# Attention operands of 73 rows without fills, laid out by dimension, with the query loads regrouped

## The chip, the cores and the metric

The kernel runs on one core of a Trainium2 chip. The metric is the time of one execution on the device in microseconds (us). The kernel before takes 661.42 us, the median of 3 runs (659.46 to 661.67). A difference of about 0.3% (2 us) is what a measurement of this kernel can tell from no change.

## The reference

One transformer layer on x of 2048 tokens x 128 features, with 16 heads of 8 dimensions. `mod` has six rows of 128 numbers, computed from a conditioning vector.

```
h = layernorm(x) * (1 + ca) + sa
v = log_map(h)                                   # per token: sqrt, arccosh, a scale
q, k, vv = v @ Wq.T, v @ Wk.T, v @ Wv.T          # 16 heads of 8
g = eta + 0.1 * tanh(tanh((h - mu) @ W1.T + b1) @ W2.T + b2)      # abs, sign kept
at = softmax((q * g) @ k.T / sqrt(8))            # per head, 2048 x 2048
x = x + ga * project(project(mu) + 0.1 * (at @ vv) @ Wo.T)
h = layernorm(x) * (1 + cb) + sb
x = x + gb * ((silu(h @ wg.T) * (h @ wu.T)) @ wd.T)
```

## The kernel before

Preparation. DVE, ACT, GpSimd and PE compute h, the log map (DVE lines L910 to L964, on a [128, 16] array of one number per token and in between with ACT's roots and Ln), the metric g, and k, v and q, in four blocks of 512 tokens (BT). The head has only 8 dimensions and the scores need more accuracy than bf16, so k and q are each split into three bf16 parts (hi, mid, lo), and all nine products of parts are summed in one matmul: the contraction runs over 3 x 3 x 8 = 72 rows.

Operands. `K_op` [128, 16 heads, 2048] holds at row 24a + 8s + i, and `Q_op` [128, 2 slots x 16 heads x 512] at row 8 (3a + s) + i, what must be multiplied for the pair of parts (a, s) and the dimension i. One row more, SHIFT_ROW = 96, carries the softmax shift in Q_op against ones in K_op. Rows 72 to 95 of K_op are filled with zeros and 96 to 127 with ones by GpSimd (`fill_k`, L357 to L363, two memsets for each group of 4 heads), and rows 64 to 127 of both slots of Q_op with zeros (L373, L386). The memsets of groups 1 to 3 of K_op and of the first slot of Q_op lie beside DVE's log map.

The way of k and q. The parts have features on the rows, h * 8 + i. They go to memory: `store_k` (L241, one transfer of 128 rows for each block and part, on SP's queue), q of block 0 in one transfer on SP's queue (L277), q of blocks 1 to 3 on GpSimd's queue (L383). Back they come by SP's queue: `load_k(g)` loads a group of 4 heads in three transfers of 24 rows, since all three parts of k stand in every set of 24; `load_q` loads all 16 heads of one block in nine transfers of 8 rows, since each part of q stands three times; `load_shift` the shift row. SP's program is in order: stores of k, wait for them all, K of group 0, store of q, wait, queries of block 0, shift, K of groups 1 to 3, then queries of block 1, and then the gathers of results.

Attention. For each of 4 blocks of queries there are 64 steps, 16 for each group of 4 heads (GH). A step (`score`, L680) computes the scores of 128 keys against 512 queries for 4 heads with 16 matmuls at L700, each 32 keys wide and over 128 rows; ACT takes exp in two instructions of 128x1024 (L522); `product` (L708) multiplies the probabilities by the values in 4 matmuls (L716). In blocks 1 to 3 the output projection and the feed-forward part of the block before are spread over the steps (AT_WO to AT_DOWN). After block 3 the last tail runs by itself. PE begins block 0 when `Q_loaded` has all ten transfers of block 0 (L777), and each group of it when `K_loaded[g]` has its three (L685).

A second pass (p = 1) recomputes everything with exact shifts if a flag asks for it. With this data it isn't taken.

Of the kernel before, what the change touches and what calls it, by code (L numbers as in the profile page):

```python
# [29 lines left out]
DH = D // H  # L30
# [9 lines left out]
SHIFT_ROW = 96  # L40
# [18 lines left out]
ONE_PAIR = float(np.array([0x3F803F80], np.uint32).view(np.float32)[0])  # L59
# [16 lines left out]
def build(nc, x, columns, wmod, fixed, w1t, w2t, w_att, wgt, wut, wdt, out):  # L76
    with ExitStack() as ctx:
# [8 lines left out]
        k_scr = nc.dram_tensor("k_scr", (H, PARTS, DH, T), BF16, kind="Internal").ap()  # L86
# [118 lines left out]
        v_done kmax_ready bound shift_ready K_filled Q_filled Q_loaded ones_ready  # L205
        scores exped pv_done o_evac norm wo_ps h2_done h2T_ps h2T_done gate_ps up_ps gate_th
        gated glu_done down_ps y_ready y_stored tail epow_in epow_out flag_in flag_ps flag_ready placed exp_table warm num_in den_in
        max_loaded shift_saved max_zero max_scores max_taken max_T""".split()
# [6 lines left out]
        K_loaded = [sem(f"K_loaded{g}") for g in range(NG)]  # L215

        def q_slot(s):

            return lambda h: Q_op[:, bass.ds(s * (H * BT) + h * BT, BT)]
# [5 lines left out]
        QUERY_LOADS = PARTS * PARTS + 1  # L225
# [3 lines left out]
        def _(sp):  # L229
# [9 lines left out]


            def store_k(b):  # L241
                for n, part in enumerate(("k_hi", "k_mid", "k_lo")):
                    sp.wait_ge(S[part], b + 1)
                    sp.dma_start(k_scr[:, n, :, b * BT:(b + 1) * BT], k_parts[b % 3][:, n, :])\
# [26 lines left out]
            sp.wait_ge(S["K_filled"], 2)  # L271
# [32 lines left out]
            def blocks(p):  # L304
                for b in range(NB):
# [3 lines left out]
                    if b + 1 < NB:  # L309
                        if not p:  # L310
                            sp.wait_ge(q_st[b + 1], 16)
                            sp.wait_ge(S["shift_ready"], b + 2)
                            sp.wait_ge(S["Q_filled"], 2)
                        sp.wait_ge(S["Q_loaded"], 16 * QUERY_LOADS * (Bk + 1))
                        if Bk:
                            sp.wait_ge(S["scores"], 2 * STEPS * Bk)
                        load_q((b + 1) % 2, b + 1, S["Q_loaded"])
                        load_shift((b + 1) % 2, b + 1, S["Q_loaded"], p)
# [11 lines left out]
            with sp.If(sp.value_load(flag_i[0:1, 0:1], min_val=0, max_val=1)):  # L330
                sp.wait_ge(S["max_zero"], 1)
                for b in range(NB):
                    sp.wait_ge(S["max_taken"], NT * GH * b + 1)
                    load_q(0, b, S["max_loaded"])
                    sp.wait_ge(S["max_loaded"], 16 * PARTS * PARTS * (b + 1))
# [9 lines left out]
        def _(pool):  # L345
# [11 lines left out]
            def fill_k(g):  # L357

                hg = slice(GH * g, GH * (g + 1))
                pool.memset(K_op[64:96, hg, :].bitcast(F32), 0.0).then_inc(S["K_filled"], 1)  # L360
                pool.wait_ge(S["K_filled"], 2 * g + 1)
                pool.memset(K_op[96:128, hg, :].bitcast(F32), ONE_PAIR).then_inc(S["K_filled"], 1)  # L362
                pool.wait_ge(S["K_filled"], 2 * g + 2)  # L363

            pool.wait_ge(S["ones_ready"], 1)
            fill_k(0)

# [5 lines left out]
            pool.memset(Q_op[64:128, 0:H * BT].bitcast(F32), 0.0).then_inc(S["Q_filled"], 1)  # L373
            pool.wait_ge(S["Q_filled"], 1)
# [3 lines left out]
            for g in range(1, NG):  # L378
                fill_k(g)
# [5 lines left out]
            pool.wait_ge(S["m2_ps"], NB)  # L385
            pool.memset(Q_op[64:128, H * BT:2 * H * BT].bitcast(F32), 0.0).then_inc(S["Q_filled"], 1)  # L386
            pool.wait_ge(S["Q_filled"], 2)
# [9 lines left out]
            with pool.If(pool.value_load(flag_i[0:1, 0:1], min_val=0, max_val=1)):  # L397

                pool.memset(Q_op[96:128, 0:H * BT].bitcast(F32), 0.0).then_inc(S["max_zero"], 1)
                with pool.Fori(NB, 2 * NB) as b:  # L400
                    tail_roots(b)
# [3 lines left out]
        def _(act):  # L405
# [54 lines left out]
            def q_split1(b):  # L460
# [4 lines left out]
                if b == 3:  # L465
                    act.wait_ge(q_st[0], 16)
# [91 lines left out]
        def _(pe):  # L558
# [121 lines left out]
            def score(Bk, j):  # L680
# [3 lines left out]
                if kt == 0 and start:  # L684
                    pe.wait_ge(K_loaded[g], 16 * PARTS)  # L685
                queries = None if isinstance(Bk, int) else q_slot(Bk % 2)
                for half_ in range(2):
# [6 lines left out]
                    for i in range(2):  # L694
                        h = GH * g + 2 * half_ + i
                        if isinstance(Bk, int):
                            q_cols = Q_op[:, (Bk % 2) * H * BT + h * BT:(Bk % 2) * H * BT + (h + 1) * BT]
                            for c in range(COLS):
                                at_ = P * kt + CW * c
                                ins = pe.matmul(slot_bank(u % 3)[CW * c:CW * (c + 1), i, :],  # L700
                                                K_op[:, h, at_:at_ + CW], q_cols, start=True, stop=True,
                                                tile_position=(0, CW * c))
                        else:
                            ins = pe.matmul(slot_bank(u % 3)[:, i, :], K_op[:, h, P * kt:P * (kt + 1)], queries(h),
                                            start=True, stop=True)
# [50 lines left out]
            def block_steps(Bk, tails):  # L756
                for j in range(STEPS):
                    score(Bk, j)
# [16 lines left out]
            def blocks(p):  # L775
                first, last = NB * p, NB * (p + 1) - 1
                pe.wait_ge(S["Q_loaded"], 16 * QUERY_LOADS * (first + 1))  # L777
                block_steps(first, False)
                if p == 0:
                    pe.wait_ge(S["ffn_ready"], 3)  # L780
                if p == 0:
                    for Bk in range(first + 1, last + 1):
                        pe.wait_ge(S["Q_loaded"], 16 * QUERY_LOADS * (Bk + 1))
                        block_steps(Bk, True)
                else:
                    with pe.Fori(first + 1, last + 1) as Bk:
                        pe.wait_ge(S["Q_loaded"], 16 * QUERY_LOADS * (Bk + 1))
                        block_steps(Bk, True)
# [34 lines left out]
            with pe.If(pe.value_load(flag_i[0:1, 0:1], min_val=0, max_val=1)):  # L823

                q_all = q_slot(0)
                with pe.Fori(0, NB) as b:
                    pe.wait_ge(S["max_loaded"], 16 * PARTS * PARTS * (b + 1))
                    for h in range(H):
                        for t in range(TPB):
                            pe.wait_ge(S["max_taken"], b * (H * TPB) + h * TPB + t + 1)  # L830
                            for i in range(NB):
                                ins = pe.matmul(bank(i), q_all(h)[:, P * t:P * (t + 1)],
                                                K_op[:, h, BT * i:BT * (i + 1)], start=True, stop=True)
# [9 lines left out]
        def _(dve):  # L843
# [22 lines left out]
            vec.did(dve.memset(ones_bf[:, :], 1.0))  # L866
# [3 lines left out]
            for b in range(NB):  # L870
# [3 lines left out]
                if b == 1:  # L874
# [4 lines left out]
                    vec.after()  # L879
                    dve.tensor_scalar(silu_b[:, :], ones_bf[:, 0:P], silu_c[:, 0:1], c_c, ALU.mult, ALU.mult)\  # L880
# [388 lines left out]
```

## Time and profile before

| | us |
|---|---|
| median of 3 runs | 661.42 |
| runs | 659.46, 661.67, 661.42 |
| the profiled execution, its own time | 658.76 |
| its span, first to last instruction | 656.6 |
| PE busy | 569.7 (87%) |
| ACT busy | 527.0 (80%) |
| DVE busy | 163.4 (25%) |
| GpSimd (POOL) busy | 56.1 (9%) |
| mean granted clock of TensorE | 0.949 |

Busy times are sums over instructions in one profiled execution; a busy PE is not PE at its peak, since matmuls are pipelined. The granted clock is a share of full speed: 1.00 is 2.4 GHz and 0.50 is 1.2 GHz. The time outside the span is 2.2 us. PE is the tensor engine, PEld its weight loads, DVE the vector engine, ACT the scalar engine, SPq and POOLq the queues on which SP and GpSimd issue transfers.

### The profile page before, as it was taken

How to read it: one execution, taken by the hardware profiler on the slowest of the kernel's cores; microseconds unless marked ns; L12 is line 12 of the kernel's file. 1: busy time of each engine (PE TensorE's matmuls, PEld its weight loads, DVE VectorE, ACT ScalarE, POOL GpSimd, SP SyncE). 2: the span in 40 equal slices, each digit the busy share in tenths (PEclk: the TensorE clock that was granted, in tenths of full speed). 3: DMA queues.
4: the chain of work that ended last, by engine and by line, in shares of the span. 5: the costliest groups of instructions: out<-in, count | busy, mean ns of one | idle time of the engine just before them, and what ended most of it. 6: DMA issues, size and time to landing. Idle time of an engine off the chain costs nothing.

```text
span 656.6 us, 14893 instructions
## 1 busy us (share of the span) xinstructions
PE 569.7 (87%) x6482; PEld 210.6 (32%) x6482; DVE 163.4 (25%) x403; ACT 527.0 (80%) x607; POOL 56.1 (9%) x33
## 2 busy tenths in 40 slices
PE   1508832999999999999999999999999999999735
PEld 0305301333333333334333333333333333433213
DVE  7995650000000035110000451100005411010174
ACT  3325461999999999889999998899999988899601
POOL 6790040000000001000000000000000000000010
PEclk9967875999999999999999999999999999999959
DMA  5001577652000033000000330000000000000000
GB/s 162 0 0 36 126 126 135 108 77 31 10 2 9 2 44 40 10 1 10 17 10 1 51 35 8 2 9 18 9 3 9 5 6 1 10 18 9 1 0 20
DMA packets 16290, 19.30 MB, mean 29 GB/s; under 512 B 2112, under 2 KB 13568, under 8 KB 16224
## 3 DMA queue, kind: packets, MB, share of 16 engines
q1 hardware_dynamic: 15600, 16.76, 15.0%
q8 instruction: 52, 0.85, 0.5%
q0 software_dynamic: 336, 1.18, 0.5%
q10 hardware_dynamic: 288, 0.40, 0.2%
q14 instruction: 14, 0.11, 0.1%
HBM read 12.10 MB, written 4.19 MB: 25 GB/s over the span
## 4 chain that ended last, share of the span: by engine, by line
PE 49%; ACT 30%; DVE 8%; issue 7%; DMA 4%; POOL 0%; ACTq 0%; SPq 0%
ACT probs L522 28%; PE ps L716 19%; PE ps L700 18%; DMA Q_op<-wmod_sb 3%; PE ps L739 2%; PE ps L744 2%; PE ps L751 2%; PE ps L593 1%; DVE probs L924 1%; PE ps L725 1%; PE ps L587 1%; PE ps L613 1%; DMA x_tm<-x_dram 1%; DVE arena L921 1%; PE ps L676 1%
## 5 line engine op out<-in xcount | busy, mean ns | idle before, releaser
L522 ACT ACTIVATE probs<-ps 128x1024 f32<-128x1024 f32 x512 | 474.0, 1084 | 41.1 <-PE ps L700 41.0
L700 PE MATMUL ps<-Q_op,K_op 128*32 128x512 bf16 x4096 | 270.3, 381 | 19.5 <-DMA Q_op<-wmod_sb 18.9
L716 PE MATMUL ps<-probs,V_op 128*32 128x512 f32 x2048 | 272.2, 603 | 1.4 <-ACT probs L522 0.8
L700 PEld LDWEIGHTS ps<-Q_op,K_op 128*32 128x32 bf16 x4096 | 116.1, 97 | 222.8 <-issue 154.6
L1065 DVE COPY O_sb<-ps 128x512 f32<-128x512 f32 x16 | 11.1, 691 | 274.3 <-PE ps L716 274.3
L716 PEld LDWEIGHTS ps<-probs,V_op 128*32 128x32 f32 x2048 | 45.0, 108 | 94.1 <-ACT probs L522 85.4
L354 POOL TENSOR_TENSOR small<-small,half 128x4 f32<-128x4 f32 x4 | 4.1, 1014 | 519.3 <-DVE small L1118 519.3
L570 PE MATMUL ps<-fixed_sb,arena 128*128 128x128 f32 x32 | 7.4, 392 | 30.6 <-DVE arena L961 19.5
L428 ACT ACTIVATE small<-small 128x16 f32<-128x16 f32 x4 | 0.9, 216 | 23.2 <-DVE small L886 7.3
L1147 DVE SCALAR_TENSOR_TENSOR arena<-arena,ps 128x512 f32<-128x512 f32 x12 | 8.2, 687 | 43.5 <-ACT arena L537 43.5
L1153 DVE TENSOR_TENSOR arena<-ps,arena 128x512 f32<-128x512 f32 x12 | 8.3, 692 | 42.3 <-PE ps L744 42.2
L1165 DVE TENSOR_TENSOR arena<-ps,mod 128x512 f32<-128x512 f32 x3 | 2.1, 692 | 63.4 <-PE ps L751 63.4
L532 ACT ACTIVATE arena<-ps 128x512 f32<-128x512 f32 x4 | 2.4, 597 | 18.6 <-PE ps L732 18.6
L570 PEld LDWEIGHTS ps<-fixed_sb,arena 128*128 128x128 f32 x32 | 5.3, 198 | 34.3 <-DVE arena L961 20.4
L362 POOL MEMSET K_op<- 32x4096 f32 x4 | 14.0, 3506 | 0.2
L360 POOL MEMSET K_op<- 32x4096 f32 x4 | 14.0, 3504 | 0.3
L676 PE MATMUL ps<-ones_bf 128*128 128x512 bf16 x16 | 7.1, 613 | 7.8 <-POOL small L354 7.8
L1088 DVE RECIPROCAL arena<-arena 128x512 f32<-128x512 f32 x4 | 13.4, 3352 | 0.1
L739 PE MATMUL ps<-arena,wg_f 128*128 128x512 f32 x24 | 13.3, 636 | 0.0
L744 PE MATMUL ps<-arena,wu_f 128*128 128x512 f32 x24 | 13.2, 631 | 0.0
L537 ACT ACTIVATE arena<-ps 128x512 f32<-128x512 f32 x12 | 7.2, 597 | 6.9 <-PE ps L739 6.9
L751 PEld LDWEIGHTS ps<-wd_f,arena 128*128 128x128 f32 x72 | 8.9, 191 | 10.1 <-issue 10.1
(154 smaller groups left out, 299.9 us busy)
## 6 DMA issues: line engine op xcount, KB each, us to landing
K_op<-k_scr SPq DMA_DIRECT2D x12, 384.0 KB
Q_op<-q_scr SPq DMA_DIRECT2D x36, 128.0 KB
arena<-O_sb SPq DMA_DIRECT2D x120, 16.0 KB
k_scr<-probs SPq DMA_DIRECT2D x9, 128.0 KB, 2.3
q_scr<-arena POOLq DMA_DIRECT2D x3, 384.0 KB, 15.5
x_tm<-x_dram SPq DMA_DIRECT2D x4, 256.0 KB, 4.6
out_dram<-arena SPq DMA_DIRECT2D x4, 256.0 KB, 2.3
wmod_sb<-wmod_dram ACTq DMA_DIRECT2D x1, 384.0 KB, 3.6
```

The source lines that it names most:

```text
L360: pool.memset(K_op[64:96, hg, :].bitcast(F32), 0.0).then_inc(S["K_filled"], 1)
L362: pool.memset(K_op[96:128, hg, :].bitcast(F32), ONE_PAIR).then_inc(S["K_filled"], 1)
L522: act.activation(probs[:, 2 * (j % 2) + half_, :], slot_bank(u % 3), ACT.Exp)\
L570: ins = pe.transpose(bank(b % 2)[:, P * t:P * (t + 1)], src[:, TPB * b + t, :], ident_sb)
L676: ins = pe.matmul(to, ones_bf[:, 0:P], ones_bf[:, 0:BT], start=True, stop=True)
L700: ins = pe.matmul(slot_bank(u % 3)[CW * c:CW * (c + 1), i, :], K_op[:, h, at_:at_ + CW], q_cols, start=True, stop=True, tile_position=(0, ...
L716: ins = pe.matmul(O_bank[32 * i:32 * (i + 1), :], V_op[:, kt, VW * h:VW * h + 32], probs[:, 2 * (j % 2) + i // 2, BT * (i % 2):BT * (i % 2 ...
L739: pe.matmul(to, wg_f[:, P * m:P * (m + 1)], h2_T, start=True, stop=True).then_inc(S["gate_ps"], 1)
L744: pe.matmul(to, wu_f[:, P * m:P * (m + 1)], h2_T, start=True, stop=True).then_inc(S["up_ps"], 1)
L751: ins = pe.matmul(to[:, P * t:P * (t + 1)], hid[:, m, P * t:P * (t + 1)], wd_f[:, m, :], start=m == 0, stop=m == NM - 1)
L1065: dve.tensor_copy(O_sb[:, g, :], O_bank).then_inc(S["o_evac"], 1)
L1088: c.did(dve.reciprocal(rec_T, rec_T))
```

## The change

All is done at once:

- The matmul of the scores takes rows 0 to 72 in place of 0 to 127 (`ROWS`, 73 in the first pass, 75 in the second). SHIFT_ROW is 72. All fills of K_op and Q_op on GpSimd are gone; the ones of K_op (rows 72 to 74) are a transfer from `ones_bf` at the start of SP's program, behind the weights.
- Features are ordered i * 16 + h, by dimension, through the host's order of the rows of Wk, Wq, W2, b2 and of the head sums. In memory k is [part, feature, token] as q is.
- The sets of rows change sides: part a of k stands three times (rows 24a + 8s + i), part s of q once in every set of 24. So `load_k` issues nine transfers of 8 rows for each group (in memory 4 heads of one dimension now lie behind each other, a run of 16 KB), and `load_q` three of 24 rows for nine of 8.
- The q of block 0 is stored in three transfers, one for each part, and loaded by head group: group 0 and the shift ahead of PE's start, each further group behind its K. PE waits for `Q_first[g]` at each group of block 0.

```
-SHIFT_ROW = 96
+SHIFT_ROW = PARTS * PARTS * DH
+ROWS = (SHIFT_ROW + 1, SHIFT_ROW + PARTS)
...
-        k_scr = nc.dram_tensor("k_scr", (H, PARTS, DH, T), BF16, kind="Internal").ap()
+        k_scr = nc.dram_tensor("k_scr", (PARTS, D, T), BF16, kind="Internal").ap()
...
+            sp.wait_ge(S["ones_bf_ready"], 1)
+            sp.dma_start(K_op[SHIFT_ROW:SHIFT_ROW + PARTS, :, :],
+                         ones_bf[0:PARTS, :].unsqueeze(1).to_broadcast([PARTS, H, T])).then_inc(S["K_ones"], 16)
...
             def load_k(g):
-                src = k_scr[GH * g:GH * (g + 1), :, :, :].rearrange("h a i t -> (a i) h t")
+                hg = slice(GH * g, GH * (g + 1))
                 for a in range(PARTS):
-                    sp.dma_start(K_op[PARTS * DH * a:PARTS * DH * (a + 1), GH * g:GH * (g + 1), :], src)\
-                        .then_inc(K_loaded[g], 16)
-
-            def load_q(slot, b, loaded):
+                    src = k_scr[a, :, :].rearrange("(i h) t -> i h t", i=DH)[:, hg, :]
+                    for s in range(PARTS):
+                        r = DH * (PARTS * a + s)
+                        sp.dma_start(K_op[r:r + DH, hg, :], src).then_inc(K_loaded[g], 16)
+
+            def load_q(slot, b, loaded, hg=slice(0, H)):
                 q3 = Q_op[:, slot * H * BT:(slot + 1) * H * BT].rearrange("p (h t) -> p h t", h=H)
-                tb = slice(b * BT, (b + 1) * BT)
-                for s in range(PARTS * PARTS):
-                    src = q_scr[s // PARTS, :, tb].rearrange("(h i) t -> i h t", i=DH)
-                    sp.dma_start(q3[DH * s:DH * (s + 1), :, :], src).then_inc(loaded, 16)
+                src = q_scr.rearrange("s (i h) t -> (s i) h t", i=DH)[:, hg, b * BT:(b + 1) * BT]
+                for a in range(PARTS):
+                    r = PARTS * DH * a
+                    sp.dma_start(q3[r:r + PARTS * DH, hg, :], src).then_inc(loaded, 16)
...
-            sp.wait_ge(S["K_filled"], 2)
...
             load_k(0)
-            sp.wait_ge(S["q_lo"], 1)
-            sp.dma_start(q_scr[:, :, 0:BT].rearrange("a f t -> f a t"), q_parts[0]).then_inc(q_st[0], 16)
-            sp.wait_ge(q_st[0], 16)
-            sp.wait_ge(S["Q_filled"], 1)
-            load_q(0, 0, S["Q_loaded"])
+            for n, part in enumerate(("q_hi", "q_mid", "q_lo")):
+                sp.wait_ge(S[part], 1)
+                sp.dma_start(q_scr[n, :, 0:BT], q_parts[0][:, n, :]).then_inc(q_st[0], 16)
+            sp.wait_ge(q_st[0], 16 * PARTS)
+            load_q(0, 0, Q_first[0], slice(0, GH))
             sp.wait_ge(S["shift_ready"], 1)
-            load_shift(0, 0, S["Q_loaded"], 0)
+            load_shift(0, 0, Q_first[0], 0)
             for g in range(1, NG):
-                sp.wait_ge(S["K_filled"], 2 * (g + 1))
                 load_k(g)
+                load_q(0, 0, Q_first[g], slice(GH * g, GH * (g + 1)))
...
-            def fill_k(g):
...
-                pool.memset(K_op[64:96, hg, :].bitcast(F32), 0.0).then_inc(S["K_filled"], 1)
...
-                pool.memset(K_op[96:128, hg, :].bitcast(F32), ONE_PAIR).then_inc(S["K_filled"], 1)
...
-            pool.memset(Q_op[64:128, 0:H * BT].bitcast(F32), 0.0).then_inc(S["Q_filled"], 1)
...
                 if kt == 0 and start:
-                    pe.wait_ge(K_loaded[g], 16 * PARTS)
+                    pe.wait_ge(K_loaded[g], 16 * PARTS * PARTS)
+                    pe.wait_ge(Q_first[g], 16 * (QUERY_LOADS if g == 0 else PARTS))
+                rows = ROWS[p]
...
-                                                K_op[:, h, at_:at_ + CW], q_cols, start=True, stop=True,
-                                                tile_position=(0, CW * c))
+                                                K_op[0:rows, h, at_k:at_k + CW], Q_op[0:rows, at_q:at_q + BT],
+                                                start=True, stop=True, tile_position=(0, CW * c))
...
+    by_dim = np.arange(D).reshape(H, DH).T.reshape(D)
```

SP's queue before, from the stores of k to the queries of block 1 (`k_scr`, `q_scr`: k and q in memory; `wmod_sb`: the shift row of a block; behind a name the rows x elements of one transfer):

```order
L244 DMA k_scr<-probs 16x8x512 x3
L251 DMA K_op<-k_scr 24x4x2048 x3
L277 DMA q_scr<-arena 128x3x512
L259 DMA Q_op<-q_scr 8x16x512 x9
L267 DMA Q_op<-wmod_sb 1x16x512
L251 DMA K_op<-k_scr 24x4x2048 x9
L259 DMA Q_op<-q_scr 8x16x512 x9
L267 DMA Q_op<-wmod_sb 1x16x512
```

The same place now:

```order
L247 DMA k_scr<-probs 128x512 x3
L257 DMA K_op<-k_scr 8x8192 x9
L282 DMA q_scr<-arena 128x512 x3
L264 DMA Q_op<-q_scr 24x4x512 x3
L272 DMA Q_op<-wmod_sb 1x16x512
L257 DMA K_op<-k_scr 8x8192 x9
L264 DMA Q_op<-q_scr 24x4x512 x3
L257 DMA K_op<-k_scr 8x8192 x9
L264 DMA Q_op<-q_scr 24x4x512 x3
L257 DMA K_op<-k_scr 8x8192 x9
L264 DMA Q_op<-q_scr 24x4x512 x3
L264 DMA Q_op<-q_scr 24x16x512 x3
```

Ahead of the first score there are nine transfers of K for three, and three of queries of a quarter of the heads for nine of all heads; the other heads' queries stand behind their K.

GpSimd before, from its fill of the values' ones to its stores of q (`V_op`: the values, `hs_bf`: the head sums in bf16):

```order
L348 MEMSET V_op 128x4352
L360 MEMSET K_op 32x4096
L362 MEMSET K_op 32x4096
L371 ISA
L371 TENSOR_TENSOR arena<-arena,mod 128x512 x4
L373 MEMSET Q_op 64x4096
L376 CAST hs_bf<-fixed_sb 128x16
L360 MEMSET K_op 32x4096
L362 MEMSET K_op 32x4096
...
L383 DMA q_scr<-arena 128x3x512 x3
L386 MEMSET Q_op 64x4096
```

GpSimd now:

```order
L351 MEMSET V_op 128x4352
L363 ISA
L363 TENSOR_TENSOR arena<-arena,mod 128x512 x4
L366 CAST hs_bf<-fixed_sb 128x16
L371 DMA q_scr<-arena 128x3x512 x3
```

Eight memsets of K_op and two of Q_op are gone; the four additions to h and the stores of q stay in their order.

## Rows read from the trace of the kernel before

**Rows 1.** The profile's chain that ended last, share of the span by engine.
```profile
PE 49%; ACT 30%; DVE 8%; issue 7%; DMA 4%; POOL 0%; ACTq 0%; SPq 0%
```
**Rows 2.** Stretches: us, busy us by engine, granted clock, DMA share, GB/s.
```profile
26.00:32.00 6.00, 5.89 (x12) 2.52 (x10) 5.93 (x14) 0.69 (x1) 5.88 (x3) 1.00 0.00 0
...
51.40:58.00 6.60, 6.56 (x15) 3.58 (x16) 3.07 (x14) 3.84 (x7) 0.00 (x0) 0.55 0.07 20
...
110.55:228.00 117.45, 117.33 (x1520) 41.06 (x1520) 2.07 (x3) 115.59 (x127) 0.00 (x0) 0.98 0.25 38
```
**Rows 3.** Chain of work in order of time: start us, us, what (0 to 52 us).
```profile
6.81 1.44 DVE silu_b L880
...
24.11 0.35 DVE arena L921
...
26.36 3.07 DVE arena L921
...
30.42 2.65 DVE small L929
...
34.05 2.59 DVE small L932
...
36.66 3.54 DVE small L934
...
40.22 0.18 DVE small L936
...
40.94 2.83 DVE small L944
...
45.28 2.05 DVE small L951
...
48.03 3.36 DVE arena L961 x4
```
**Rows 4.** Timeline of GpSimd: start us, us, instruction.
```profile
8.22 3.51 POOL L362 MEMSET K_op<- 32x4096 f32 x1
...
25.62 3.51 POOL L373 MEMSET Q_op<- 64x4096 f32 x1
...
29.53 3.50 POOL L360 MEMSET K_op<- 32x4096 f32 x1
33.09 3.51 POOL L362 MEMSET K_op<- 32x4096 f32 x1
```
**Rows 5.** Timeline, SP's queue and PE, from K's first load on.
```profile
75.24 1.17 SPq L251 DMA_DIRECT2D K_op<-k_scr  x3
79.51 0.40 SPq L277 DMA_DIRECT2D q_scr<-arena  x1
85.68 3.19 SPq L259 DMA_DIRECT2D Q_op<-q_scr  x9
...
88.92 1.54 SPq L267 DMA_DIRECT2D Q_op<-wmod_sb  x1
...
88.59 3.11 PE L676 MATMUL ps<-ones_bf 128*128 128x512 bf16 x7
```
**Rows 6.** Chain of work in order of time, ahead of the first score.
```profile
88.92 21.39 DMA Q_op<-wmod_sb
```
**Rows 7.** Stretches, columns as in rows 2, for the transfers.
```profile
76.00:84.00 8.00, 7.14 (x16) 2.06 (x14) 4.10 (x8) 3.96 (x7) 0.00 (x0) 0.88 0.79 169
...
98.00:102.00 4.00, 0.00 (x0) 0.00 (x0) 0.00 (x0) 0.00 (x0) 0.00 (x0) 0.50 0.85 69
...
112.00:134.00 22.00, 22.00 (x279) 7.53 (x272) 0.00 (x0) 21.30 (x24) 0.00 (x0) 0.92 0.68 114
134.60:152.00 17.40, 17.36 (x228) 6.16 (x228) 0.69 (x1) 17.40 (x21) 0.00 (x0) 1.00 0.58 71
```
**Rows 8.** Matmuls of one line: count, ns min/median/max, first and last start.
```profile
L636 PE MATMUL ps<-arena,hs_bf x4: 379/382/590, 79.4 to 88.1; 128*16 128x512 bf16 x4
...
L700 PE MATMUL ps<-Q_op,K_op x4096: 376/379/634, 110.6 to 615.2; 128*32 128x512 bf16 x196
```

More of the change, by code:

```diff
@@ L58 @@
 DOWN_BANK = (0, 3, 6, 7)
-ONE_PAIR = float(np.array([0x3F803F80], np.uint32).view(np.float32)[0])
 class Chain:
@@ L215, in build @@
         K_loaded = [sem(f"K_loaded{g}") for g in range(NG)]
+        Q_first = [sem(f"Q_first{g}") for g in range(NG)]
         def q_slot(s):
-            return lambda h: Q_op[:, bass.ds(s * (H * BT) + h * BT, BT)]
+            return lambda h, rows: Q_op[0:rows, bass.ds(s * (H * BT) + h * BT, BT)]
         def row3(m, n):
@@ L377, in _ @@
             pool.wait_ge(S["hs_ready"], 1)
-            for g in range(1, NG):
-                fill_k(g)
             for b in range(1, NB):
@@ L677, in keep_warm, with score @@
                 ins.then_inc(S["warm"], 1)
-            def score(Bk, j):
+            def score(Bk, j, p):
                 start = isinstance(Bk, int) and Bk == 0
@@ L696, in score @@
                         if isinstance(Bk, int):
-                            q_cols = Q_op[:, (Bk % 2) * H * BT + h * BT:(Bk % 2) * H * BT + (h + 1) * BT]
+                            at_q = (Bk % 2) * H * BT + h * BT
                             for c in range(COLS):
-                                at_ = P * kt + CW * c
+                                at_k = P * kt + CW * c
                                 ins = pe.matmul(slot_bank(u % 3)[CW * c:CW * (c + 1), i, :],
-                                                K_op[:, h, at_:at_ + CW], q_cols, start=True, stop=True,
-                                                tile_position=(0, CW * c))
-                        else:
-                            ins = pe.matmul(slot_bank(u % 3)[:, i, :], K_op[:, h, P * kt:P * (kt + 1)], queries(h),
-                                            start=True, stop=True)
+                                                K_op[0:rows, h, at_k:at_k + CW], Q_op[0:rows, at_q:at_q + BT],
+                                                start=True, stop=True, tile_position=(0, CW * c))
+                        else:
+                            ins = pe.matmul(slot_bank(u % 3)[:, i, :], K_op[0:rows, h, P * kt:P * (kt + 1)],
+                                            queries(h, rows), start=True, stop=True)
                     ins.then_inc(S["scores"], 1)
@@ L754, in t_down, with block_steps @@
                     ins.then_inc(S["down_ps"], 1)
-            def block_steps(Bk, tails):
+            def block_steps(Bk, tails, p):
                 for j in range(STEPS):
-                    score(Bk, j)
+                    score(Bk, j, p)
                     if j:
@@ L776, in blocks @@
                 first, last = NB * p, NB * (p + 1) - 1
-                pe.wait_ge(S["Q_loaded"], 16 * QUERY_LOADS * (first + 1))
-                block_steps(first, False)
+                if p == 0:
+                    pe.wait_ge(S["K_ones"], 16)
+                else:
+                    pe.wait_ge(S["Q_loaded"], 16 * QUERY_LOADS * first)
+                block_steps(first, False, p)
                 if p == 0:
@@ L831, in _ @@
                             for i in range(NB):
-                                ins = pe.matmul(bank(i), q_all(h)[:, P * t:P * (t + 1)],
-                                                K_op[:, h, BT * i:BT * (i + 1)], start=True, stop=True)
+                                ins = pe.matmul(bank(i), q_all(h, SHIFT_ROW)[:, P * t:P * (t + 1)],
+                                                K_op[0:SHIFT_ROW, h, BT * i:BT * (i + 1)], start=True, stop=True)
                             ins.then_inc(S["max_scores"], 1)
@@ L864, in newton @@
                 vec.after()
-            vec.did(dve.memset(ones_bf[:, :], 1.0))
+            dve.memset(ones_bf[:, :], 1.0).then_inc(S["ones_bf_ready"], 1)
             vec.did(dve.memset(ok[:, :, :], 1.0))
@@ L1243 @@
     mu[0] = 1.0
-    heads = np.repeat(np.eye(H, dtype=np.float32), DH, axis=0)
+    heads = np.repeat(np.eye(H, dtype=np.float32), DH, axis=0)[by_dim]
     lay = {
         "x": a["L0_attn_x"][0],
-        "columns": np.concatenate([a["L0_attn_b1"].reshape(MH, P).T, a["L0_attn_b2"].reshape(D, 1), eta, -mu,
+        "columns": np.concatenate([a["L0_attn_b1"].reshape(MH, P).T, a["L0_attn_b2"].reshape(D, 1)[by_dim], eta, -mu,
                                    a["L0_c"].reshape(D, 1)], axis=1),
```

43 lines of the change are left out of this document (17 added, 26 removed).

## The prediction

> **What bounds the kernel now.** I read the chain of waits first, because a share of busy time says nothing about a start that everything waits for. The chain [rows 1] gives PE 49% and ACT 30%: once attention runs, these two hand score tiles to each other and nothing else matters. In block 0 PE is busy for 117.33 of 117.45 us [rows 2], so a group of 4 heads takes 117.45 / 4 = 29.4 us, and nothing that the change does to a transfer can shorten this, it can only be late for it. Ahead of it lie 110.55 us of preparation, all of it on the path. Two stretches of it concern the change.
>
> The first is a DVE chain from 26.4 to 51.4 us. Among its pieces [rows 3], six stand out: `tensor_scalar` on 128x16 numbers takes 2.65, 2.59, 3.54, 2.83 and 2.05 us, where the `scalar_tensor_tensor` of the same size (L936) takes 0.18; and L921 takes 3.07 us for its last block and 0.35 for the one before. GpSimd's rows [rows 4] say why: the fill of Q_op ends at 29.13, L921 at 29.43; the first two of the six fills of K_op that follow back to back, 3.5 us each, end at 33.03 and 36.60, L929 at 33.07 and L932 at 36.64. Counting on, the others end at 40.2, 43.7, 47.3 and 50.8; L934 ends at 40.20, L944 at 43.77, L951 at 47.33. Each long DVE instruction ends within 0.3 us, mostly 0.04, of the end of a fill. DVE is held by the fills, one whole fill after another.
>
> The second is the chain of transfers from K in memory to the first score [rows 5]: K of group 0 is asked for at 75.24, the first queries are stored at 79.51, loaded from 85.68, and the shift row, issued at 88.92, lands 21.39 us later with all that is queued ahead of it. PE then waits for this alone [rows 6].
>
> **The fills go.** Replace each held instruction by its free duration, 0.18 us for 128x16 (L936) and 0.35 for L921 [rows 3]: L921 gives 2.72, L929 2.47, L932 2.41, L934 3.36, L944 2.65, L951 1.87. For L961 the 16 multiplications end at 53.7 and the first four at 51.39, so 12 free ones take 2.3 us, four 0.8, and the held four give 2.6. Sum 18.1 us. What is late next: ACT's root, table load and Ln follow L944 too, and the held L951 hides them today. DVE needs 1.5 us from L944's end to L951 in any case [rows 3], and more behind it; I count ACT as just covered (1 us as the bound). At the start L880 ends at 8.25 with the K_op fill that ends at 8.23 [rows 4]; it should take 0.2 of its 1.44, which brings the modulation matmuls and their readers forward by 1.2 us, no more, because the last x tiles arrive at about the same time (0 and 1.4 as bounds).
>
> Then v is ready 19.3 us earlier, at 32.1, just behind PE's first metric matmuls, which fill 26 to 32 us today [rows 2]. Before, PE came to this point from idleness at a granted clock of 0.55, near the 1.2 GHz level; in 26 to 32 us it had 1.00. With no gap it should stay at 2.4 GHz, and L613 and L593 in the first 6.6 us get shorter. ACT's tanh and copies take most of that back; I take 1.0 us (bounds 0 and 3). **Front: 18.1 + 1.2 + 1.0 = 20.3 us.** K of group 0 is then asked for at 75.24 - 20.3 = 54.9.
>
> **The loads.** A K group was three transfers of 24 rows, 1.18 MB, and moves in 76 to 84 us with 0.79 of the DMA engines busy [rows 7], about 12 of 16. It is now nine of 8 rows. No K row shows that shape, but the query loads before have just these rows, 8 at a time from row 0 to row 71, and the same 1.18 MB: the one that runs by itself (134.6 to 152) keeps 0.58 busy, about 8 of 16 with the small gathers beside it, and takes 18 us at 71 GB/s [rows 7]. So: at least 12 us if an engine keeps the pace it had with 24 rows and only their number falls (8 x 12/8); 18 as the query loads; with packets of 16 KB instead of 1 KB there is less per packet to save but longer blocking. I take 20.5 us, nearer the query loads than the 12, and keep 12 to 26.
>
> The Trainium skill, "DMA: Bandwidth & Descriptors", on why a semaphore counts 16, says that a transfer runs on the largest number up to 16 that divides both sides' slowest dimension: 8 engines for 8 rows, 12 for 24. The shares 0.58 and 0.79 agree. The skill, "SBUF — State Buffer", section on the DMA port swizzle, speaks against this change: 8 neighbouring rows reach two of 16 ports, 24 reach six; an estimate from its 436 GB/s is 21.7 us for a K group, and by it the total would be 1 us longer than mine.
>
> Behind K the rest of the start is: the query store shares the queues of engines that still carry K, so it lands after K. Before, K ended at 84 and the query loads began at 85.68: 1.7 us. Storing in three parts changes nothing, since K holds them. Then three loads of one head group (nine issues took 3.19 us, so three take 1.1), the shift's issue of 1.54 and about 1.9 to land: 4.5 us, in which 0.3 MB arrive on 12 engines. GpSimd's stores of blocks 1 to 3 (1.2 MB) fall in the middle of K; from 98 to 102 us, where both kinds met before, only 69 GB/s moved [rows 7]. I take 1 us for it (0 to 4). From K's request to the first score: 0.8 + 20.5 + 1.7 + 4.5 + 1.0 = 28.5 us, against 35.3 before (75.24 to 110.55). **Gain 6.8 us; first score at 83.4.** PE's warming matmuls ended at 91.7 [rows 5], now at 71.4, so no engine is late for it.
>
> **Later groups.** Their K loads (20.5 us) and the query loads of the group (about 2.5) now stand in one queue: 23 us for each 29.4 us group, 6 us of cover each time. If a group takes more than 29.4, PE stands still three times. The queries of block 1 follow as three loads, with 35 us left before block 1. The waits added (Q_first, one per group) hold nothing that would run otherwise. SP issues 36 transfers ahead of the gathers of block 0, which are wanted only in block 1. The ones row of K (3 rows, 0.2 MB) goes out behind the weights, 45 us ahead of its use: nothing.
>
> **73 rows instead of 128.** L636 fills 16 columns of the array and takes 0.382 us, L700 fills 32 and takes 0.379 [rows 8]: the time is that of 512 moved columns. No row has fewer than 128 rows of contraction. I take zero; a gain is possible where PE paces the blocks, a loss I exclude, as not one more column is moved. By the skill ("TensorE: Matmul & The Clock Gate", on packing) a matmul of few rows takes as long as a full one.
>
> **Sum.** 20.3 + 6.8 = 27.1 us. The profiled execution took 658.8, so 631.7; it is the lowest of the four times and 2.7 under the median of the three (661.4), which would give 634.3. I say 633.
>
> **Rivals.**
> (a) The transfers are not held by the rows they write: an engine keeps its pace, K takes 12 us instead of 20.5. For: fewer, longer packets. Against: the query loads, 18 us in the same walk. The first score comes 8.5 us earlier: 624. Chance 0.12.
> (b) DVE is not held by the fills, or something else takes their place (ACT's tables, a wait on PE). Then only the transfers gain: 633 + 18 = 651. For: only that ends coincide. Against: seven coincidences within 0.3 us, and free twins in the same chain. Chance 0.06.
> (c) The slower one: K loads collapse. From 112 to 134 us 12 engines moved only 114 GB/s [rows 7], against 169 for the first group; the same loss on 8 engines would be 71 x 114 / 169 = 48 GB/s, 25 us a group with 2.5 for queries: still under 29.4. It takes a K group of x us to change the total by -20.3 + (x + 8 - 35.3) + 3 (x + 2.5 - 29.4), which is zero at x = 32 (37 GB/s). At 34 us it is +7: 668. Against: no stretch of 8-row loads shows less than 69. Chance 0.05; between 27 and 32 us (no change to -10) another 0.08, in which within 0.3% is 0.04.
> (d) The reordering by dimension has a price that I missed, in the k stores or in the head sums; all keep their shapes, and a tensor of 128 rows is stored as before. It is within the range.
>
> My forecast keeps 0.69. **Range.** K at 12 us without contention gives 623; K at 26 us and 4 us of contention 642; I take 622 to 645, which leaves out (b), (c) and tails. **Chances.** About 0.3% is what a measurement of this kernel can tell from no change (2 us). Faster 0.91, the same 0.04, slower 0.05.
>
> **What would show it.** In the profile after: the 128x16 `tensor_scalar` near 0.2 us; v ready near 32 us and a PE clock of 1.00 behind it; K of group 0 asked for near 55; a DMA share near 0.5 while K loads, some 20 us long; first score near 83; one group every 29.4 us with no wait of PE for DMA in block 0. If the first score is near 75, (a) is right. If the DVE pieces stay long, (b). If PE waits for DMA at the start of groups 1 to 3, (c). If a group takes other than 29.4 us with no wait in it, the 73 rows did something after all.

## The result, and the profile after

The changed kernel takes 625.36 us, the median of 4 runs (622.84 to 626.72), against 660.92 before (the median of all 4 of its runs; three of them gave the 661.42 above): a ratio of 0.946 with a 95% interval of 0.9424 to 0.9496. It is faster by 35.6 us, 7.6 us below the forecast of 633 and inside the range of 622 to 645. The profiled execution took 624.65 us (span 622.8) against 658.76 (span 656.6).

The chain of the changed kernel, by engine, against [rows 1]:

```profile
PE 50%; ACT 33%; issue 8%; DVE 5%; DMA 3%; SPq 1%; POOL 0%; ACTq 0%
```

DVE's share falls from 8% to 5%. The chain of work in order of time (start us, us, what) shows where it went; DVE's line numbers are ten lower than before (L934 here is L944 there), and the rows answer to [rows 3]:

```profile
6.91 0.36 DVE silu_b L870
...
25.42 0.35 DVE arena L911
...
26.76 0.19 DVE small L919
...
27.92 0.19 DVE small L922
...
28.13 0.19 DVE small L924
...
29.05 0.19 DVE small L934
...
29.50 1.28 ACT L425
```

The held pieces of 128x16 are at 0.19 us, the 128x512 one (L911) at 0.35 and the 128x128 one (L870) at 0.36. DVE's timeline has the last of them and the start of the scaling of v:

```profile
30.76 0.17 DVE L941 TENSOR_SCALAR small<-small 128x16 f32<-128x16 f32 x1
30.97 0.25 DVE L943 RECIPROCAL small<-small 128x16 f32<-128x16 f32 x1
31.26 0.17 DVE L946 SCALAR_TENSOR_TENSOR small<-small 128x16 f32<-128x16 f32 x1
```

L946 reads Ln, which ACT has ready at 31.01: covered, by 0.25 us. The chain itself runs on ACT from 29.50 on: the table load for Ln, then from 31.02 to 33.58 another table load and two copies (L404), and only then the copy of v (L429) that PE waits for. The clock, which had been 1.00 in 26 to 32 us before, was low there and rose just ahead of v (stretches, columns as in [rows 2]):

```profile
26.00:32.00 6.00, 5.71 (x8) 1.90 (x6) 5.07 (x33) 3.60 (x7) 0.00 (x0) 0.61 0.00 0
32.40:39.00 6.60, 5.58 (x23) 3.09 (x24) 3.34 (x17) 5.49 (x10) 0.00 (x0) 1.00 0.07 25
```

SP's queue and GpSimd from K's first load on (timeline), against [rows 5]:

```profile
54.42 3.83 SPq L257 DMA_DIRECT2D K_op<-k_scr  x9
58.30 1.31 SPq L282 DMA_DIRECT2D q_scr<-arena  x3
72.95 1.17 SPq L264 DMA_DIRECT2D Q_op<-q_scr  x3
74.16 0.63 SPq L272 DMA_DIRECT2D Q_op<-wmod_sb  x1
...
75.72 1.63 POOL L371 DMA_DIRECT2D q_scr<-arena  x2 [8.42 <-DVE arena L977]
```

K of group 0 is asked for at 54.42 (75.24 before). And the chain just ahead of the first score, with PE's part of the timeline, where [rows 6] had one wait for the shift:

```profile
59.16 13.77 DMA q_scr<-arena
...
73.02 0.63 ACT arena L451
73.64 0.53 ACT arena L452
...
74.22 0.59 PE ps L620
74.81 3.10 PE ps L660 x7
77.91 0.88 PE ps L686 x8
```

This is a wait that the prediction did not name. ACT's split of the queries of block 3 reuses the buffer of block 0 and so waits for the store of block 0's queries, which stands behind K on the queues. ACT is idle for 8.0 us, then come PE's last head sum, seven warming matmuls, and the first score at 77.84, with no wait for the query loads. The stretches, K's loads first, and last the first 5 us of scores in the kernel before:

```profile
55.20:71.20 16.00, 7.21 (x17) 2.00 (x15) 7.18 (x13) 7.09 (x12) 0.94 (x1) 0.80 0.57 107
77.80:82.80 5.00, 4.37 (x61) 1.45 (x64) 0.67 (x5) 4.54 (x7) 0.00 (x0) 0.93 0.76 129
77.84:195.00 117.16, 116.41 (x1528) 40.22 (x1528) 2.70 (x8) 116.70 (x129) 0.00 (x0) 1.00 0.29 57
...
110.50:115.50 5.00, 4.95 (x40) 1.74 (x44) 0.00 (x0) 3.77 (x4) 0.00 (x0) 0.51 0.76 129
```

So the 33.8 us of span are: 20.8 up to K's request (75.24 to 54.42), 11.9 from there to the first score (35.3 to 23.4), and 1.1 behind it (546.0 to 545.0), where the first 5 us have a clock of 0.93 instead of 0.51. PE never waits for a transfer in block 0 or later.

### The profile page after: what moved, and what is told of

Same layout as the page of the kernel before. It is cut to its first block, busy times and chain, and to the rows that moved or that the text cites. A ratio compares the mean times of both kernels' runs of the same rounds, so it can differ in the third digit from the quotient of the medians.

```text
span 622.8 us, 14892 instructions
## 1 busy us (share of the span) xinstructions
PE 565.1 (91%) x6482; PEld 207.4 (33%) x6482; DVE 144.4 (23%) x403; ACT 526.5 (85%) x607; POOL 20.1 (3%) x23
## 3 DMA queue, kind: packets, MB, share of 16 engines
q0 software_dynamic: 336, 1.18, 0.6%
## 4 chain that ended last, share of the span: by engine, by line
PE 50%; ACT 33%; issue 8%; DVE 5%; DMA 3%; SPq 1%; POOL 0%; ACTq 0%
ACT probs L506 30%; PE ps L702 19%; PE ps L686 19%; DMA q_scr<-arena 2%; PE ps L725 2%; PE ps L730 2%; PE ps L737 2%; PE ps L660 1%; DVE probs L914 1%; PE ps L711 1%; DMA x_tm<-x_dram 1%; PE ps L597 1%; PE ps L603 1%; SPq L257 1%; PE ps L577 1%
## 5 line engine op out<-in xcount | busy, mean ns | idle before, releaser
L686 PE MATMUL ps<-Q_op,K_op 73*32 73x512 bf16 x4096 | 269.4, 379 | 1.0 <-ACT probs L506 1.0
L686 PEld LDWEIGHTS ps<-Q_op,K_op 73*32 73x32 bf16 x4096 | 114.7, 96 | 204.5 <-issue 135.2
L620 PE MATMUL ps<-arena,hs_bf 128*16 128x512 bf16 x4 | 1.7, 434 | 10.9 <-ACT arena L452 10.9
L737 PE MATMUL ps<-wd_f,arena 128*128 128x128 f32 x72 | 11.2, 292 | 0.0
L451 ACT ACTIVATE arena<-arena 128x512 bf16<-128x512 f32 x4 | 2.5, 622 | 10.3 <-DMA q_scr<-arena 8.0
L711 PE MATMUL ps<-w_att_sb,arena 128*128 128x128 f32 x32 | 5.5, 326 | 5.7 <-DVE arena L1082 5.7
```

Of the source, the lines that this page charges most:

```text
L711: ins = pe.matmul(M_bank[:, P * t:P * (t + 1)], att_T[:, P * t:P * (t + 1)], wo_sb, start=True, stop=True)
L737: ins = pe.matmul(to[:, P * t:P * (t + 1)], hid[:, m, P * t:P * (t + 1)], wd_f[:, m, :], start=m == 0, stop=m == NM - 1)
```

## The experiments

Every group of kernels was timed beside the kernel before on its chip (658.85 to 660.05 us there); the table has, from each profiled execution, when K of group 0 is asked for, the first score, and the rest of the span behind it. The four runs below "changed" shared one chip, the next three another, and the last four a third. In the code, `...` stands for lines left out, and the `.then_inc` behind a transfer is left out too.

| run | us | ratio to before (95%) | K asked for | first score | rest |
|---|---|---|---|---|---|
| before | 661.42 | 1 | 75.24 | 110.55 | 546.0 |
| changed | 625.36 | 0.946 (0.9424 to 0.9496) | 54.42 | 77.84 | 545.0 |
| fills_alone | 637.85 | 0.9685 (0.9637 to 0.9734) | 55.07 | 89.06 | 546.5 |
| fills_kept | 646.16 | 0.9798 (0.976 to 0.9836) | 74.87 | 98.87 | 544.6 |
| by_head_grouped | 621.96 | 0.9431 (0.9394 to 0.9467) | 55.97 | 72.35 | 545.9 |
| fourth_buffer | 628.74 | 0.9532 (0.9495 to 0.9568) | 54.62 | 78.94 | 547.9 |
| spread_rows | 620.62 | 0.9401 (0.9368 to 0.9435) | 54.40 | 71.72 | 547.9 |
| by_head_fourth_buffer | 621.82 | 0.945 (0.9385 to 0.9516) | 55.04 | 71.49 | 548.0 |
| by_head_spread | 624.35 | 0.9474 (0.9443 to 0.9506) | 55.15 | 74.14 | 547.7 |
| changed_again | 624.58 | 0.9458 (0.9421 to 0.9494) | 54.35 | 77.84 | 545.0 |
| spread_warm | 618.61 | 0.9365 (0.9329 to 0.9402) | 55.24 | 72.63 | 544.6 |
| spread_warm_held | 618.63 | 0.9368 (0.9331 to 0.9404) | 54.38 | 72.30 | 545.1 |
| fourth_buffer_held | 625.66 | 0.9479 (0.9441 to 0.9517) | 54.50 | 76.95 | 546.9 |

### The fills: one part done alone, and one part undone

fills_alone is the kernel before with 73 rows and no fills; all transfers have their old shape and order, and the ones come by a transfer. In outline, not word for word:

```
 def load_k(g):        # as before: three loads of 24 rows
 def load_q(...):      # as before: nine loads of 8 rows, all heads at once
-    pool.memset(...)  # all fills
+    sp.dma_start(K_op[SHIFT_ROW:SHIFT_ROW + PARTS, :, :], ones ...)
```

> The kernel before with one part of the change: operands of 73 rows and no fills; layout by head, K in three loads of 24 rows, queries in nine of 8, first queries in one piece. My theory (the fills held DVE): K of group 0 is asked for near 54.4 us as in the changed kernel (before 75.2), the way from there to the first score stays 35 us, so the first score near 90 and the profiled time near 638. Rival (the front's gain comes from the new layout or the transfers): K is asked for near 75 and the time stays near 659.

fills_kept is the changed kernel with nine memsets where they were, on rows nobody reads:

```
+            def fill_k(g):
+                for _ in range(2):
+                    fill(K_op[96:128, GH * g:GH * (g + 1), :])
...
+            fill(Q_op[96:128, 0:H * BT])
```

> The changed kernel with nine memsets of GpSimd put back at their old places and sizes (on rows 96 to 127, which nobody reads). Theory: DVE's tensor_scalar pieces take 2 to 3.5 us again, K of group 0 is asked for near 75, time near 645 (20 more than the changed kernel). Rival (DVE is not held by fills): pieces stay near 0.2 us, time 625.

The first came to 637.85 us with K asked for at 55.07, the second to 646.16 us with K asked for at 74.87. DVE's and GpSimd's timelines in fills_kept:

```profile
26.29 3.14 DVE L927 TENSOR_SCALAR arena<-arena 128x512 f32<-128x512 f32 x1
30.43 2.65 DVE L935 TENSOR_SCALAR small<-small 128x16 f32<-128x16 f32 x1
34.06 2.58 DVE L938 TENSOR_SCALAR small<-small 128x16 f32<-128x16 f32 x1
36.67 3.53 DVE L940 TENSOR_SCALAR small<-small 128x16 f32<-128x16 f32 x1
40.95 2.82 DVE L950 TENSOR_SCALAR small<-small 128x16 f32<-128x16 f32 x1
...
29.54 21.32 POOL L363 MEMSET K_op<- 32x4096 f32 x6
```

The same instructions are held for the same times as in [rows 3], though the fills have nothing to do with them and the 73-row matmul and all transfers are those of the changed kernel. The fills held DVE, and they cost 20 us of the front. This is shown both ways, with the fills taken out of the kernel before and put back into the changed one; rival (b) falls.

### The layout by dimension

by_head_grouped gives the layout by head back and keeps everything else:

```
-                src = k_scr[a, :, :].rearrange("(i h) t -> i h t", i=DH)[:, hg, :]
-                for s in range(PARTS):
-                        sp.dma_start(K_op[r:r + DH, hg, :], src)
+                src = k_scr[GH * g:GH * (g + 1), :, :, :].rearrange("h a i t -> (a i) h t")
+                sp.dma_start(K_op[PARTS * DH * a:PARTS * DH * (a + 1), GH * g:GH * (g + 1), :], src)
...
-                for a in range(PARTS):
+                for s in range(PARTS * PARTS):
```

> The changed kernel with the layout by head given back (K in three loads of 24 rows a group, queries in nine of 8 rows), but still no fills, first queries stored by part and loaded by head group. Theory (8-row K loads cost 16.4 us where 24-row ones cost 8; the grouping gave the gain of the start): K of group 0 lands near 63, queries of the group near 70, first score near 71.5, time near 619: the new layout by dimension is a loss of 5 to 6 us at the start. Rival (the layout by dimension pays): the first score at 78 or later, time 625 or more.

The first score came at 72.35, 5.5 us earlier than in the changed kernel, the time was 621.96. Its timeline and the stretch of K's loads:

```profile
55.97 1.27 SPq L254 DMA_DIRECT2D K_op<-k_scr  x3
57.29 3.31 SPq L280 DMA_DIRECT2D q_scr<-arena  x3
66.13 3.03 SPq L262 DMA_DIRECT2D Q_op<-q_scr  x9
...
56.70:64.70 8.00, 7.15 (x16) 2.02 (x14) 4.02 (x8) 3.96 (x7) 0.00 (x0) 0.87 0.79 174
```

K moves at 174 GB/s in place of 107, the queries are asked for at 66.13 in place of 72.95. In the profiles the layout by dimension costs 5.5 us at the start and 4.6 of the span (622.8 against 618.2). Here PE no longer waited for a transfer or the queries' store: the first score followed ACT's splits, the head sums and the warming matmuls, so 5.5 us is what this path left of the faster K. In the times the intervals of the ratios overlap (0.9394 to 0.9467, 0.9424 to 0.9496), and the two were not timed on one chip, so the size in time is open; that it gains nothing is shown. K was also asked for 1.5 us later here than in the changed kernel. That time lies between 54.35 and 55.97 over the kernels without fills, and 55.24 is by dimension (spread_warm), so the layout alone doesn't explain it; it stays open. by_head_grouped against fills_alone, both by head and with no fills, prices the grouping of the first queries: first score 72.35 against 89.06, 15.9 us in time.

### What holds an 8-row load: its engines, or where its rows lie

spread_rows keeps 8-row K loads of 16 KB a row, and changes only the row at which the pair (a, s) and dimension i stand:

```
-                        r = DH * (PARTS * a + s)
-                        sp.dma_start(K_op[r:r + DH, hg, :], src)
+                        r = a + PARTS * DH * s
+                        sp.dma_start(K_op[r:r + PARTS * (DH - 1) + 1:PARTS, hg, :], src)
...
-                    sp.dma_start(q3[r:r + PARTS * DH, hg, :], src)
+                    sp.dma_start(q3[a:r:PARTS, hg, :], src)
```

> The changed kernel with the 72 rows in another order: the pair of parts (a, s) and dimension i at row a + 24 s + 3 i, so that a K load still has 8 rows, 16 KB each, on the same engines, but the rows lie three apart (over 22 rows) and a query load has 24 rows three apart. Theory of the rows (where the rows lie in SBUF holds the load): K of group 0 lands in 9 to 12 us instead of 16, the query store with it, time 619 to 622. Theory of the engines (eight engines at their own pace): K takes 16 us, time 625.

It took 620.62 us. The queries were asked for at 66.21 instead of 72.95, and the stretch of K's loads (columns as in rows 2) is

```profile
55.20:64.20 9.00, 6.82 (x16) 1.91 (x14) 5.95 (x12) 6.25 (x11) 0.00 (x0) 1.00 0.51 159
```

No more engines are busy (0.51 here, 0.57 in the changed kernel; both stretches hold stores of queries too), and they move 159 GB/s instead of 107. What changed is where the eight rows lie. The Trainium skill, "SBUF — State Buffer", section on the DMA port swizzle, counts 4 neighbouring rows to a port: 8 neighbouring rows share two ports, eight rows three apart reach six. The run agrees that the rows' places decide. An estimate from the Trainium skill's figures for two ports, 54 GB/s, is too low for the changed kernel: 1.18 MB of K in 16 us are 74 GB/s (the 107 of the stretch include the stores of queries). Nine loads stand in one queue there and go to other rows one after another; whether that makes the difference was not tried.

by_head_spread does the same to the layout by head (24 rows over 70, query loads of 8 rows over 22), on top of the fourth buffer:

> The same with the rows three apart in K loads (24 rows over 70) and in query loads (8 rows over 22). Theory of the rows: K of group 0 in 5 to 7 us instead of 8, queries of the group in 2 to 3 instead of 4.5; the first score then only waits for ACT and PE, near 71, time 618 to 619. Theory of the engines: both as in by_head_fourth_buffer, same time.

This one missed twice: 624.35 us, and the first score came 2.7 us later than without it. K, expected in 5 to 7 us instead of 8, was no faster: the queries were asked for at 65.19 against 65.01, and 56 to 64 us moved 186 GB/s against 187. For loads of 24 rows the places of the rows brought nothing on balance; their three issues took 2.47 us against 1.28, and what the transfers alone gained is not separated from that. The delay of the first score lies in the query loads. Its timeline, and that of the same kernel with neighbouring rows, for nine query loads and the shift:

```profile
65.19 6.59 SPq L264 DMA_DIRECT2D Q_op<-q_scr  x9
71.82 0.60 SPq L272 DMA_DIRECT2D Q_op<-wmod_sb  x1
```

```profile
65.01 3.03 SPq L263 DMA_DIRECT2D Q_op<-q_scr  x9
68.08 0.59 SPq L271 DMA_DIRECT2D Q_op<-wmod_sb  x1
```

A query load of 8 rows three apart takes SP 0.73 us to issue instead of 0.34. With nine of them ahead of the first score that is 3.6 us; with three of 24 rows, as in spread_rows, 1.3 us (2.44 against 1.17). K's nine issues there took 5.97 us against 3.83; whether that delayed anything behind K's own transfers was not tried.

### The wait that took over

fourth_buffer gives block 3's queries the place of the shift parts, which only the second pass uses:

```
+        q_parts.append(tmp(PARTS * BT // 2, PARTS, BT, dt=BF16))
+        shift_parts = q_parts[3][0:H, :, :]
...
-                if b == 3:
-                    act.wait_ge(q_st[0], 16 * PARTS)
```

> The changed kernel with a fourth buffer for the parts of q (that of the shift parts, used in the second pass only), so that ACT's first split of block 3 no longer waits for the store of block 0. In the changed kernel ACT waits 8.0 us for it and the first score follows by way of ACT, PE's head sums and the seven warming matmuls. Theory A (this wait sets the start): ACT is done near 68, the first score comes when the query loads land, up to 1.5 us earlier, time 623 to 625. Theory B (the query loads land as late as that way): first score unchanged at 77.8, PE waits for a transfer and starts at the low clock, time 625 to 626.

Slower than both had it: 628.74 us. ACT no longer waits, but the first score comes at 78.94, with PE waiting 9.0 us for the shift row. The stretches from the query loads on show two things:

```profile
73.50:78.90 5.40, 0.00 (x0) 0.00 (x0) 0.00 (x0) 0.00 (x0) 0.00 (x0) 0.50 0.62 168
78.90:83.90 5.00, 4.96 (x40) 1.75 (x44) 0.00 (x0) 3.77 (x4) 0.00 (x0) 0.50 0.68 92
83.90:88.90 5.00, 5.00 (x52) 1.87 (x48) 0.00 (x0) 2.99 (x4) 0.00 (x0) 0.70 0.66 101
```

The first steps run at 0.50 and 0.70, where the changed kernel, whose head sum and warming matmuls end right at the first score, had 0.93 and 1.00. And the query loads take 5.4 us to land: GpSimd's stores of blocks 2 and 3 are no longer held back by ACT's wait and stand beside them. The next kernel tests the second, with one wait on GpSimd that holds all three of its stores:

```
+            pool.wait_ge(Q_first[0], 16 * QUERY_LOADS)
             for b in range(1, NB):
                 pool.wait_ge(S["q_lo"], b + 1)
```

> fourth_buffer (8-row K loads, neighbouring rows, no wait of ACT), with GpSimd's stores held back until the first group's queries have landed. In fourth_buffer the queries were asked for at 73.5 and landed at 78.9. Theory (the stores, no longer held back by ACT's wait, delay them): the first score comes 1 to 2 us earlier, near 77.3, still at the low clock, time 626.5 to 627.5. Rival (they land at 78.9 anyway): 628.7.

The first score came 2.0 us earlier, at 76.95, and the time was 625.66. So the stores cost 2.0 us of the landing, and the low clock 2 to 3: the rest of the span was 546.9 here and 547.9 in fourth_buffer, against 545.0.

by_head_fourth_buffer is the same edit with the layout by head:

> Layout by head, no fills, first queries by head group, and the fourth buffer for the parts of q. If the first score is set by ACT and PE there (head sums and warming matmuls end near 71), as I expect, the time is that of by_head_grouped, near 619, within 1. If the store of the queries still held ACT, 2 us less.

621.82 us, as by_head_grouped: the first score is 0.9 us earlier, and the rest 2.1 longer, again at the low clock. One of its runs was 627.79, so its interval is wide.

### The best version

> The changed kernel itself once more, on the chip of the next three: near 625, first score near 77.8 with the clock rising at once (remainder of the span 545 us).

The repeat gave 624.58 us, first score 77.84, a granted clock of 0.93 and 1.00 in the first 10 us: in both profiled executions the clock rose at the same place. spread_warm is spread_rows with more warming matmuls, which leave PE no gap over 1.7 us between 64 us and the first score, and none right before it:

```
+            for b in range(1, NB):
+                if b == 3:
+                    pe.wait_ge(S["m2_sb"], NB)
+                    keep_warm(6, M_bank)
+                nq(b)
...
-            keep_warm(7, M_bank)
+            keep_warm(16, M_bank)
```

> spread_rows with 6 warming matmuls ahead of PE's last head sum (a gap of 2.5 us) and 16 instead of 7 ahead of the first score, so that PE works without a gap up to it. In spread_rows the first score came at 71.7 and the rest of the span took 547.9 us at a granted clock of 0.50 and 0.73 in its first 10 us; in the changed kernel the rest took 545.0 with 0.93 and 1.00. Theory (the low clock costs these 3 us): first score at 71.5 to 72.5, the rest 545, time 617 to 619. Rival (the 3 us come from transfers beside the first steps, not from the clock): the clock is high and the time stays near 621.

618.61 us, faster than the kernel before and, on one chip, 6.0 us faster than the changed kernel (624.58). Against spread_rows it is 2.0 us, on another chip and with overlapping intervals, so in time that gain is open. The stretches around the first score at 72.63, and then two of spread_rows with PE's timeline at its first score:

```profile
64.00:66.50 2.50, 1.35 (x3) 0.29 (x3) 1.96 (x4) 2.49 (x4) 0.00 (x0) 1.00 0.29 102
66.50:71.70 5.20, 4.66 (x21) 1.89 (x22) 4.40 (x8) 5.18 (x10) 2.54 (x3) 1.00 0.42 129
71.70:76.70 5.00, 4.37 (x57) 1.47 (x59) 1.15 (x6) 4.44 (x6) 0.03 (x1) 1.00 0.74 265
```

```profile
71.70:76.70 5.00, 4.98 (x40) 1.70 (x44) 0.03 (x2) 3.77 (x4) 0.00 (x0) 0.50 0.60 209
76.70:81.70 5.00, 5.00 (x56) 1.96 (x52) 0.00 (x0) 3.14 (x4) 0.00 (x0) 0.73 0.60 146
...
71.72 3.60 PE L686 MATMUL ps<-Q_op,K_op 73*32 73x512 bf16 x32 [0.54 <-DMA Q_op<-wmod_sb]
```

The clock stays at 2.4 GHz (1.00), the transfers beside the first steps are no slower (229 GB/s in the 5 us from the first score, 206 in spread_rows), and still the rest falls from 547.9 to 544.6. It falls at the beginning: in the first 20 us of scores PE finished 257 matmuls instead of 228, and the later blocks agree. So the 3 us in the profile were the clock. In spread_rows a gap of 0.54 us, a wait for the shift row, parted PE's warming matmuls from the first score, and the clock stayed at 0.50 until about 79 us. In the changed kernel nothing parted them, and it rose 0.7 us behind the first score.

> spread_warm, and GpSimd's stores of the queries of blocks 1 to 3 wait until the queries of the first group have landed. Theory (these stores stand beside the first query loads and delay them): queries and shift land 0.5 to 1.5 us earlier, time 0.5 to 1 us under spread_warm. Rival: no difference within 0.3%.

No difference, 618.63 us: there the first score waits for PE's warming matmuls, which end at 72.3, and not for a load.

## Why the prediction was right, and where its sizes were off

**The fills: right.** Forecast 18.1 + 1.2 + 1.0 = 20.3 us up to K's request, measured 20.8: 18.0 in DVE's chain, 0.9 ahead of it, and 1.9 behind PE's first matmul on v (23.8 us before, 21.9 now). The held pieces came to their free durations. The start hides one that the prediction did not list, the 128x16 `tensor_scalar` at L886 (9.95 us, 1.81 long, 0.17 now), which ended with the fill of 8.22; and the fill said to end at 8.23 ended at 8.16. For the part on PE's clock the result was right and half of the argument: in 32.4 to 39 us the granted clock was 1.00, where [rows 2] had 0.55, but it did not stay up from before. In 26 to 32 us it was 0.61 now and 1.00 before, and it rose just ahead of v.

**The K loads: right mechanism, 4.5 us too dear.** The term was 20.5 us for nine 8-row loads. From 0.8 us behind the request to 1.7 us ahead of the landed store, as the sum counted it, it was 16.0 (55.2 to 71.2). I leaned on the query loads of the same walk, 18 us, and went above them for blocking by 16 KB packets; K came in below 18. Whether the long packets did that was not tried. By its numbers rival (a) did better than the forecast: 12 us for K is 4.0 off and 20.5 is 4.5, its total of 624 is 1.4 off and 633 is 7.6, and the first score at 77.84 lies nearer to its 75 than to 83.4. Its reason is what fails: it had the transfers not held by the rows they write, and spread_rows shows that they are (159 GB/s against 107). That its total came so near is luck: its K was 4.0 us too cheap, and the stores (1.0), the clock (1.1) and the front (0.5) made up for much of that.

**The contention: 1.0 us that did not come.** GpSimd's stores of blocks 2 and 3 were to meet the loads. ACT's wait held them back until 75.7, out of the way. Without this wait GpSimd's stores cost 2.0 us (fourth_buffer against fourth_buffer_held), inside the term's bounds of 0 to 4, but on the query loads and not in the middle of K (the queries were asked for at 73.49 and 73.40).

**The end of the start chain: right number by luck, wrong path.** Forecast 4.5 us from the landed store to the first score; it took 4.9. But it ran through ACT's buffer wait, the head sum and the warming matmuls, not through the query loads. "No engine is late for it" was the false sentence: I compared the end of the warming matmuls (71.4) with the first score and did not see that a store that moves from ahead of ACT's need to 8 us behind it holds the matmuls. That wait stood in the kernel's text all along (on `q_st[0]`, at ACT's split of block 3).

**The clock at the first steps: missed.** Because of that path PE had worked up to the first score, the clock rose some 4 us earlier in the block than before, and the rest of the span was 1.1 us shorter.

Together: 4.5 for K, 1.0 for the contention, 0.5 for the front, 1.1 for the clock, less 0.4 at the end of the start chain, and 0.3 of time outside the span (2.2 before, 1.9 now): 7.0 us between the forecast gain of 27.1 and the 34.1 of the profiled executions. All but one of the errors lie on the same side, which is why the forecast came out 7.6 us too slow. Rival (c) has a slip: by its own formula a K group of 27 us gives -20 and not -10, and no run came near it. Later groups and the queries of block 1 were covered, as forecast (no wait, 117.16 us for the block). The 73 rows cost and gave nothing: the matmul took 379 ns at 73 rows, and

```profile
L686 PE MATMUL ps<-Q_op,K_op 73*32 73x512 bf16 x4096 | 269.4, 379 | 1.0 <-ACT probs L506 1.0
```

answers to [rows 8].

## What to carry to other kernels

When small DVE instructions are long, lay the other engine's timeline beside them: if they end where its fills end, the fill is the cost, and rows that are never filled because the matmul doesn't take them are free. Split a change into its parts before keeping it: of three here, no fills gave 22 us and grouping the first queries some 16, while the new layout gave nothing. And when a transfer moves later, look for every engine that reuses its source buffer, and look at the clock at which the waiting engine starts again.

## What the runs showed of the hardware

- A GpSimd memset of 3.5 us held `tensor_scalar` instructions of DVE in SBUF for up to 3.4 us, as small as 128x16, but not `scalar_tensor_tensor` or `reciprocal` on 128x16: L936 ran at 40.22, inside the fill of 40.21 to 43.7, in 0.18 us [rows 3], and the reciprocal of L859 at 33.34, inside the fill of 33.09 to 36.60, in 0.25 us. The Trainium skill, "SBUF — State Buffer", on the shared port pair, says that DVE takes this pair in its two-port modes, and for two SBUF inputs only against a GpSimd instruction that reads; a memset reads nothing. The traces agree.
- Loads of eight rows three apart instead of neighbours brought 159 GB/s instead of 107 on the same number of engines (spread_rows), and in by_head_spread 0.73 instead of 0.34 us of SP's time for the issue of a query load. Loads of 24 rows gained nothing by it on balance (186 against 187 GB/s, issues included).
- A removed wait made the kernel slower by 3 to 4 us (fourth_buffer), through the clock of TensorE (2 to 3 us over the first steps) and through stores that it had held back (2.0 us).
- After a short gap of PE the clock can stay at its low level: with none before the first score it rose 0.7 us behind it (changed kernel, two executions), with a gap of 0.54 us only 7.7 us behind it (spread_rows), though PE had been at work again since 67.5 us there and since 74.2 in the changed kernel. That the gap made the difference was not tried alone.
